# Cross-attention and routed experts on one core: exponentials per head on ScalarE, and both halves of the expert weights split with one pass fewer, the low half on VectorE

## The reference

```
x = x + softmax(mask(Wq·LN(x) · (Wk·ctx)^T / 8)) · (Wv·ctx) · Wo + bo        16 heads of 64
h = LN(x);  s = sigmoid(h·gate^T + bias);  the two largest of 9 experts per token, weights normalised
x = x + sum over the two experts e:  cw[e] · (silu(h·w1[e]^T) * (h·w3[e]^T)) · w2[e]^T     hidden width 704
```

## Time and profile before

| | us |
|---|---|
| median of 3 runs | 498.68 |
| lowest, highest | 497.95, 504.11 |
| the profiled execution | 499.68 |
| its span, first to last instruction | 497.8 |

### The profile page before, as it was taken

How to read it: one execution, slowest core, us unless ns; L and a number is a source line. 1 busy time by engine, 2 the same in 40 slices (tenths; PEclk the granted TensorE clock), 3 DMA queues, 4 the chain that set the end, 5 groups by cost and what they waited for, 6 DMA issues and landing times.

```text
span 497.8 us, 11324 instructions
## 1 busy us (share of the span) xinstructions
PE 409.8 (82%) x3049; PEld 310.2 (62%) x3049; DVE 315.9 (63%) x714; ACT 242.2 (49%) x402; POOL 294.5 (59%) x269
## 2 busy tenths in 40 slices
PE   2868769999999998721139999999999999999970
PEld 3758347786686686611015777777777777777750
DVE  5883689998898888459954745455545545544430
ACT  2877257877777783187214343334334333343310
POOL 0232166988988987374733655676666666666232
PEclk9979889999999999965557999999999999999986
DMA  8902773465466465245223878999999999999751
GB/s 264 339 4 85 232 244 111 136 193 201 134 191 200 135 182 181 69 130 154 69 69 81 158 137 135 142 141 139 133 150 132 142 144 139 137 137 155 113 82 22
DMA packets 112610, 71.45 MB, mean 144 GB/s; under 512 B 82940, under 2 KB 106172, under 8 KB 112572
## 3 DMA queue, kind: packets, MB, share of 16 engines
q1 hardware_dynamic: 104892, 60.43, 53.2%
q0 software_dynamic: 7680, 10.49, 13.9%
HBM read 39.02 MB, written 12.22 MB: 103 GB/s over the span
## 4 chain that ended last, share of the span: by engine, by line
PE 52%; DVE 15%; DMA 12%; POOL 8%; issue 6%; ACT 4%; SPq 1%; POOLq 1%; DVEq 0%; ACTq 0%
PE ps L611 29%; PE ps L624 14%; DMA out_rows<-work 8%; POOL w_all L1134 4%; POOL work L1146 2%; PE ps L479 2%; PE ps L448 2%; DVE work L878 2%; DVE work L1051 1%; DMA w_all<-in_wk 1%; PE ps L528 1%; DVE work L885 1%; DMA w_all<-b_rows 1%; DVE work L900 1%; PE ps L592 1%
## 5 line engine op out<-in xcount | busy, mean ns | idle before, releaser
L611 PE MATMUL ps<-w_all,work 128*128 x960 | 152.2, 316 | 8.9 <-DMA work<-work 8.9
L611 PEld LDWEIGHTS ps<-w_all,work 128*128 128x128 f16 x960 | 94.9, 99 | 57.1 <-issue 9.1
L1206 POOL DMA_INDIRECT out_rows<-work x40 | 64.1, 1602 | 57.7 <-DMA out_rows<-work 21.4
L1087 DVE SCALAR_TENSOR_TENSOR work<-ps,work 128x352 f32<-128x352 f32 x80 | 42.0, 524 | 70.7 <-PE ps L611 70.7
L624 PE MATMUL ps<-w_all,work 128*128 x680 | 82.1, 276 | 2.7 <-DMA work<-work 2.7
L1134 POOL TENSOR_TENSOR w_all<-stage,w_all 128x1088 f16<-128x1088 f32 (+1 forms) x32 | 74.5, 2333 | 6.8 <-ACT w_all L702 6.8
L1194 POOL DMA_INDIRECT work<-xn_rows,work x40 | 58.5, 1462 | 33.2 <-POOL work L1191 32.2
L624 PEld LDWEIGHTS ps<-w_all,work 128*128 128x128 f16 x680 | 67.2, 99 | 14.4 <-issue 2.9
L779 ACT ACTIVATE work<-work 128x704 f16<-128x704 f32 x40 | 31.6, 790 | 77.3 <-DVE work L1087 77.3
L528 PE MATMUL ps<-w_all,work 128*128 128x256 f16 (+1 forms) x480 | 55.1, 273 | 9.2 <-DVE work L910 9.2
L773 ACT ACTIVATE work<-ps 128x352 f32<-128x352 f32 x80 | 36.9, 464 | 46.9 <-PE ps L611 46.5
(11 more groups left out here) (135 smaller groups left out, 575.5 us busy)
## 6 DMA issues: line engine op xcount, KB each, us to landing
stage<-in_wt SPq DMA_DIRECT2D x36, 544.0 KB, 4.2
work<-in_x SPq DMA_DIRECT2D x32, 128.0 KB, 4.3
b_rows<-w_all SPq DMA_DIRECT2D x4, 616.0 KB
w_all<-b_rows SPq DMA_DIRECT2D x2, 1152.0 KB, 5.8
out_rows<-work SPq DMA_DIRECT2D x17, 128.0 KB, 5.0
xn_rows<-work SPq DMA_DIRECT2D x17, 128.0 KB, 4.3
w_all<-in_x SPq DMA_DIRECT2D x1, 2048.0 KB, 15.6
work<-work SPq DMA_TRANSPOSE x80, 3.4
```

What stands on the lines that cost most here:

```text
L611: mm = pe.matmul(ps[:, c, 0:half], xt[:, par, block, :], weights(wbase + off, half), start=(k == 0 and n == 0), stop=(k == KD - 1 and n == 2))
L1087: dve.scalar_tensor_tensor(out=sg[:, par, c * HID // 2:(c + 1) * HID // 2], in0=ps[:, 2 + c, 0:HID // 2], scalar=1.0 / SP_W, in1=sg[:, par ...
L1206: pool.indirect_dma_start(out=acc, out_offset=bass.IndirectOffsetOnAxis(ap=ids[:, par], axis=0), in_=yb[:, par], in_offset=None, compute_o ...
```

## The change

For the experts 0 to 5 ScalarE now writes the high half straight from the loaded chunk, in one pass with scale 64 (`w_direct`), and does not scale `stage` in place. The low half, 64 times `stage` minus high half, is made by VectorE in one instruction (`w_rest`), two per step in steps 4 to 15, behind `normalise2` and ahead of `logits`. GpSimd's two `w_low` per step are gone from the token loop; for the experts 6 and 7 the old way stays.

VectorE no longer subtracts the maxima from the scores. It multiplies them by -1/8 (`nmx`, three instructions of 128 x 6 or 128 x 4). ScalarE makes the exponentials from PSUM, head by head: 16 instructions of 128 x 77 with the head's column of `nmx` as bias and an accumulator output that gives the head's sum. VectorE's sum over `ebuf` is gone; its reciprocal stays. The score banks are released by the exponentials.

```diff
--- before.py
+++ after.py
@@ -153,6 +153,7 @@
         xn2b, o = view(work, o, [2, D], F32)
         xn2t, o = view(work, o, [2, KD, P], F32)
         mx, o = view(work, o, [2, HEADS], F32)
+        nmx, o = view(work, o, [2, HEADS], F32)
         rs, o = view(work, o, [2, HEADS], F32)
         rr, o = view(work, o, [2, HEADS], F32)
         st6, o = view(work, o, [2, 6], F32)
@@ -247,8 +248,8 @@
         x_in, xr_in = sems("x_in", 2), sems("xr_in", 2)
         x1_out, xn2_out = sems("x1_out", 2), sems("xn2_out", 2)
         xn_ok, xt_mm, xh_ok, xl_ok, sc_mm = (sem(n) for n in ("xn_ok", "xt_mm", "xh_ok", "xl_ok", "sc_mm"))
-        max_ok, sub_ok, exp_ok, sum_ok, rec_ok, norm_ok = (sem(n) for n in (
-            "max_ok", "sub_ok", "exp_ok", "sum_ok", "rec_ok", "norm_ok"))
+        max_ok, neg_ok, exp_ok, rec_ok, norm_ok = (sem(n) for n in (
+            "max_ok", "neg_ok", "exp_ok", "rec_ok", "norm_ok"))
         pt_mm, ph_ok, pl_ok, out_mm, xb_ok, x1_ok = (sem(n) for n in ("pt_mm", "ph_ok", "pl_ok", "out_mm", "xb_ok", "x1_ok"))
         st_ok, mv_ok, ve_ok, rstd_ok, xn2_ok = (sem(n) for n in ("st_ok", "mv_ok", "ve_ok", "rstd_ok", "xn2_ok"))
         xn2t_mm, xn2t_ok, gate_mm, lg_ok = (sem(n) for n in ("xn2t_mm", "xn2t_ok", "gate_mm", "lg_ok"))
@@ -497,7 +498,7 @@
                 pe.wait_ge(xl_ok, i + 1)
                 h0 = 0
                 for c, nh in enumerate(SC_H):
-                    at_least(pe, sub_ok, 3 * i + (c - 2))
+                    at_least(pe, exp_ok, 3 * i + (c - 2))
                     w = nh * J
                     dst = ps[:, c, 0:w]
                     pe.matmul(dst.rearrange("p (h j) -> p h j", j=J), idb[:],
@@ -698,8 +699,13 @@
                     act.wait_ge(w_in[part], e * 16 + 16)
                     act.activation(stage[:, part, :], stage[:, part, :], ACT.Copy, scale=SP_W).then_inc(w_sc_ok, 1)
                 for part in parts:
-                    act.wait_ge(w_sc_ok, e * 4 + (part + 1))
+                    act.wait_ge(w_sc_ok, (e - EARLY) * 4 + (part + 1))
                     act.activation(w_chunk(e, part, 0), stage[:, part, :], ACT.Copy).then_inc(w_hi_ok, 1)
+
+            def w_direct(e, parts):
+                for part in parts:
+                    act.wait_ge(w_in[part], e * 16 + 16)
+                    act.activation(w_chunk(e, part, 0), stage[:, part, :], ACT.Copy, scale=SP_W).then_inc(w_hi_ok, 1)
 
             def x_high(i, par):
                 act.wait_ge(xt_mm, i + 1)
@@ -707,8 +713,17 @@
                 act.activation(x_h[:, par], ps[:, 7, 0:D].rearrange("p (k t) -> p k t", k=KD), ACT.Copy).then_inc(xh_ok, 1)
 
             def exp(i, par):
-                act.wait_ge(sub_ok, 3 * i + 3)
-                act.activation(ebuf[par][:, 0:HJ], ebuf[par][:, 0:HJ], ACT.Exp, scale=DH ** -0.5).then_inc(exp_ok, 1)
+
+                at_least(act, pt_mm, 3 * (i - 1))
+                at_least(act, rec_ok, i - 1)
+                h = 0
+                for c, nh in enumerate(SC_H):
+                    act.wait_ge(neg_ok, 3 * i + (c + 1))
+                    for k in range(nh):
+                        ins = act.activation(ebuf[par][:, h * J:(h + 1) * J], ps[:, c, k * J:(k + 1) * J], ACT.Exp,
+                                             bias=nmx[:, par, h:h + 1], scale=DH ** -0.5, accum_out=rs[:, par, h:h + 1])
+                        h += 1
+                    ins.then_inc(exp_ok, 1)
 
             def p_high(i):
                 at_least(act, out_mm, i)
@@ -737,7 +752,7 @@
                     for b in range(B):
                         act.wait_ge(b_out[b], 16 * 2)
                 if on_w(n):
-                    w_high((s - W_STEP) // 2, chunk_parts(n))
+                    w_direct((s - W_STEP) // 2, chunk_parts(n))
                 if on(n, LAG_G):
                     gate_copy(s - LAG_G, (n - LAG_G) % 2)
                 if on(n, 0):
@@ -879,18 +894,20 @@
 
             def shift(i, par):
 
-                at_least(dve, pt_mm, 3 * (i - 1))
+                at_least(dve, exp_ok, 3 * (i - 1))
                 for c, (h0, nh, src) in enumerate(score_banks()):
                     dve.wait_ge(max_ok, 3 * i + (c + 1))
-                    dve.tensor_tensor(ebuf[par][:, h0 * J:(h0 + nh) * J].rearrange("p (h j) -> p h j", j=J), src,
-                                      mx[:, par, h0:h0 + nh].unsqueeze(2).to_broadcast([P, nh, J]),
-                                      ALU.subtract).then_inc(sub_ok, 1)
+                    dve.tensor_scalar(nmx[:, par, h0:h0 + nh], mx[:, par, h0:h0 + nh], -DH ** -0.5, None,
+                                      ALU.mult).then_inc(neg_ok, 1)
+
+            def w_rest(e, parts):
+                for part in parts:
+                    dve.wait_ge(w_hi_ok, e * 4 + (part + 1))
+                    dve.scalar_tensor_tensor(out=w_chunk(e, part, 1), in0=stage[:, part, :], scalar=SP_W,
+                                             in1=w_chunk(e, part, 0), op0=ALU.mult, op1=ALU.subtract).then_inc(w_lo_ok, 1)
 
             def sums(i, par):
-                dve.wait_ge(exp_ok, i + 1)
-                dve.tensor_reduce(rs[:, par], ebuf[par][:, 0:HJ].rearrange("p (h j) -> p h j", j=J), AX.X,
-                                  ALU.add).then_inc(sum_ok, 1)
-                dve.wait_ge(sum_ok, i + 1)
+                dve.wait_ge(exp_ok, 3 * i + 3)
                 at_least(dve, norm_ok, i - 1)
                 dve.reciprocal(rr[:, par], rs[:, par]).then_inc(rec_ok, 1)
 
@@ -959,6 +976,8 @@
                     normalise(s + 2, n % 2)
                 if on(n, LAG_XN2):
                     normalise2(s - LAG_XN2, (n - LAG_XN2) % 2)
+                if on_w(n - 1):
+                    w_rest((s - 1 - W_STEP) // 2, chunk_parts(n - 1))
                 if on(n, LAG_G):
                     logits(s - LAG_G)
                 if n in B_STEPS:
@@ -1158,12 +1177,8 @@
             def step(s, n):
                 if on(n, 2):
                     bias(s - 2, n % 2)
-                if on_w(n - 1):
-                    w_low((s - 1 - W_STEP) // 2, chunk_parts(n - 1)[0])
                 if on(n, 1):
                     norm(s - 1, (n - 1) % 2)
-                if on_w(n - 1):
-                    w_low((s - 1 - W_STEP) // 2, chunk_parts(n - 1)[1])
                 if n in B_STEPS:
                     b_low(n - B_STEPS[0])
                 if n == LATE_SPLIT + 2:
```

## The result

| | before | changed |
|---|---|---|
| median, us | 498.86 (4 runs) | 544.07 (4 runs, 543.49 to 545.99) |
| profiled execution's span, us | 497.8 | 542.3 |
| mean granted TensorE clock | 0.923 | 0.907 |

The ratio is 1.0889, 95% interval 1.0809 to 1.0969: the change makes the kernel slower by 45 us.

A forecast was written before the change was run, and what follows sets the result against it. TensorE was taken as nearly the bound, 8.87 of 9.24 us a step, waiting for residual behind a store. After the change: 499.68 + 34.6 (ring) + 1.2 (steps 1 to 3) = 535.5, forecast 535 us, range 519 to 556.

The forecast's parts named there:

- the ring: Token loop: residual, VectorE's low halves, weight loads, store, next residual; bounds each of 12 steps, +34.6 us in all.
- the first steps: Steps 1 to 3, set by ScalarE: 3 x 0.4 = 1.2 us slower, at most 11.
- First part of the ring: VectorE from residual to the end of both low halves: 2.15 + 0.40 + 0.79 + 2.47 = 5.81 us.
- the third rival: GpSimd holds up VectorE's w_rest by 0.4 to 1.2 us per step, 10 us in all: 545 us; chance 0.10.
- Second part: SyncE's queue and store, low halves' end to next residual: 6.56 us in hardware loop, 5.8 in written-out steps, 6.31 mean.
- my lower end: ScalarE's exponentials overlap and start every 0.12 us, 1.9 us per tile.
- my upper end: ScalarE reads each exponential's accumulator with an extra instruction: 0.49 us each, 7.8 us per tile.
- ScalarE's ring: Residual, maxima and first product, exponentials, probabilities' split, halves of x, next residual: 8.8 us, costing nothing in steps 4 to 15.
- The first one: SyncE's weight loads don't hold up the store; TensorE's 8.87 us a step bounds, 495 us; chance 0.05.
- The second: ScalarE becomes the bound at 0.6 us an exponential, 13.9 us a step: 572 us; chance 0.03.
- The fourth: TensorE's clock falls in its new waits, about 14.9 us a step: 568 us; chance 0.04.
- the row with 3.09 us: Earlier trace row: a TensorE wait of 3.09 us left the granted clock at 1.00, so it should hold.

The follow-up runs named there:

- cut in two different ways: Changed kernel with VectorE's low halves first in its step: 511.64 us; changed kernel with SyncE's store ahead of the weight loads: 514.16 us.
- one reordering: Changed kernel with only SyncE's queue reordered, the weight loads issued one step later, behind that step's store: 514.16 us, ratio 1.0247.
- the full reordering: Kernel before with SyncE's weight loads behind the store of x1 and ahead of the store of the normalised rows: 494.16 us, ratio 0.9866.
- the first reordering tried there: Kernel before with SyncE's two weight loads behind both stores of the step, ahead of the residual tile's load: 503.61 us, ratio 1.0051.

## Why the prediction was right, and where its sizes were off

I said 535 us, range 519 to 556, slower with 0.93; it is 544.07. The mechanism, the ring, holds: it is in the chain, it is cut in two different ways with the same result, and it is there without the exponentials. The sum is 9 us short of the profiled execution (544.35): 4.0 us in the ring, 3.5 in the first steps and 1.2 behind step 16, where I had nothing (from `residual` of step 16 to that of step 17 it takes 8.55 us in place of 7.03; I did not look for the cause).

**First part of the ring, 5.81 us forecast.** It comes to 149.45 less the twelve second parts (77.3 us), over 12: 6.01 us. VectorE in step 7 and step 8:

```profile
134.19 0.30 DVE L900 TENSOR_SCALAR work<-work 128x6 f32<-128x6 f32 x3
134.45 0.18 DVE L939 BATCH_NORM_AGGREGATE work<-work 128x2 f32<-128x6 f32 x1
135.56 3.02 DVE L906 SCALAR_TENSOR_TENSOR w_all<-stage,w_all 128x1088 f32 x2
...
147.37 0.29 DVE L900 TENSOR_SCALAR work<-work 128x6 f32<-128x6 f32 x3
...
148.70 2.49 DVE L906 SCALAR_TENSOR_TENSOR w_all<-stage,w_all 128x1088 f32 x2
```

The three products took 0.30, not 0.40, but in the hardware loop VectorE also idles 0.24 us ahead of L874, which I had not counted; up to the low halves it is 3.35 us on average, as forecast (3.34). The two low halves took 2.49 in eight steps, as forecast (2.47), and 3.02 in steps 4 to 7. That is the third rival, in part: GpSimd's bias sum had just started in step 7, and in step 8 it started just after VectorE.

```profile
135.50 0.73 POOL L1169 TENSOR_TENSOR work<-work,bo_b 128x256 f32<-128x256 f32 x1
...
148.84 2.93 POOL L1169 TENSOR_TENSOR work<-work,bo_b 128x256 f32<-128x256 f32 x1
```

Step 6 is like step 7. In steps 4 and 5 the sum started 0.46 us into the first low half, got its turn between the two and held up the second:

```profile
97.31 1.41 POOL L1169 TENSOR_TENSOR work<-work,bo_b 128x256 f32<-128x256 f32 x1
98.05 1.82 DVE L906 SCALAR_TENSOR_TENSOR w_all<-stage,w_all 128x1088 f16<-128x1088 f32 x1
```

Together it cost 4 x 0.53 = 2.1 us. The Trainium skill, page "SBUF — State Buffer", section "SBUF: two separate sides", says that the first of the two keeps the other out for its whole instruction. Steps 7 and 4 agree: VectorE loses 0.53 us to a sum that takes 0.73. In step 8 the sum lasts 2.93 us and ends 0.58 after VectorE's second low half, so it was kept out for two instructions, where the rule speaks of one. What decides between the two cases no run shows.

**Second part, 6.31 forecast.** 77.3 / 12 = 6.44 us: 6.6 in the hardware loop as said, 6.17, 6.26, 5.86 and 6.06 at the written-out steps where I took 5.8. Together with the first part 12 x 0.33 = 4.0 us, +38.6 in place of +34.6.

**The first steps, +1.2 forecast: the mis-sized term.** They cost 4.7 us. An exponential costs 0.30 us, near the 0.28 taken (the 0.12 of my lower end stood on no row), but it is two instructions, as my upper end had it (ScalarE, order of time):

```profile
147.88 0.32 ACT L723 ACTIVATE w_all<-ps,work 128x77 f32<-128x77 f32 x1
148.08 0.20 ACT L723 ACTIVATION_READ_ACCUMULATOR w_all<-ps,work 128x1 f32 x1
148.18 0.32 ACT L723 ACTIVATE w_all<-ps,work 128x77 f32<-128x77 f32 x1
```

What I had too short was ScalarE's ring: step 3 to step 4 takes 93.72 - 83.90 = 9.82 us, not 8.8. From `residual` to the first exponential it is 2.4 us (2.3 taken), the exponentials take 4.8 (4.5), and from ScalarE's split at 91.12 to the next `residual` it is 2.6, where I had 2.0. The slower exponentials count from tile 1 on, so that `residual` of step 3 is already 83.90 - 80.62 = 3.3 us late. This last number is rough: `residual` of step 3 starts at 82.17 to 84.30 in the six traces with the accumulators, and at 80.62 to 82.37 in the five with the exponentials as before, 1.8 us apart on average. So of the 4.7 us some 3.2 are the exponentials' and the rest may be the difference of one trace from another. Without the accumulators step 3 to step 4 takes 8.36 us.

**The rivals.** The first one (not slower) had the store free of the low halves; it is not. The second needed 0.49 us an exponential; it is 0.30. The third cost 2.1 us where I had 10. The fourth: I said the clock would stay at 1.00. It did not. These are a wait and the `project` behind it, twice (columns as in the earlier trace rows):

```profile
155.72:158.55 2.83, 0.00 (x1) 0.01 (x1) 0.72 (x2) 1.27 (x2) 0.00 (x0) 0.91 0.28 101
158.55:163.00 4.45, 4.45 (x28) 3.44 (x29) 4.21 (x12) 2.94 (x20) 2.41 (x3) 0.67 0.10 29
143.07:145.94 2.87, 0.00 (x1) 0.01 (x1) 0.72 (x2) 1.38 (x2) 0.00 (x0) 1.00 0.17 62
145.94:149.00 3.06, 3.06 (x28) 2.75 (x29) 2.82 (x11) 1.44 (x11) 1.03 (x3) 1.00 0.14 43
```

After one wait of 2.8 us the granted clock was 0.67, part of the stretch at the lower of the two levels (1.2 and 2.4 GHz), after another of the same length 1.00. Of the twelve waits for `residual` in steps 5 to 16, eight were followed by such a fall (the waits 2.1 to 4.6 us), four were not (1.3 to 2.9 us), so the length of the wait alone does not decide it. The Trainium skill, page "TensorE: Matmul & The Clock Gate", section "HAM oscillation — how this bites in real kernels", which I had set aside for the row with 3.09 us, describes such falls after waits for DMAs that come back in every turn; the waits in its example are longer than most here. The fall cost nothing here: the step from 157.83 with the slow `project` took 12.55 us, the one from 145.22 with the fast one 12.61. That TensorE's spare 3.3 us took it up fits this.

## What to carry to other kernels

Before moving work from one engine to another, ask not only whether the new engine has the time, but what stands ahead of the work in its order and what waits for its result: here 2.5 us of work moved behind the one instruction that waits for a store, while the queue of that store waits for the work. That made a ring of two lines of code that never name each other. A queue that serves several engines in order carries every wait to all that is behind it, and its order is the cheapest thing to change: one reordering took back 30 of the 45 us, and in the kernel before, the full reordering gave 1.3%. But the first reordering tried there only put another wait in front; read what each entry of the queue waits for.

## What the runs showed of the hardware that was not expected

- A VectorE instruction with two SBUF inputs and a GpSimd one kept each other out: 0.73 us of GpSimd's work took 2.93 us beside two low halves when VectorE was just ahead, and 1.41 us when it started later in the first of them and got in between; the low halves took 3.02 in place of 2.49 us when GpSimd was first or got in between.
- An exponential of 128 x 77 with accumulator output is an ACTIVATE and a read of the accumulator, 0.30 us for both, 4.8 us for 16, against 1.23 us for one ACTIVATE of 128 x 1232. Without the accumulator output 16 of them took 3.55 us.
- The granted clock fell after some waits of TensorE of 2.1 to 2.9 us that came back every 12.5 us or so, and not after others of 1.3 to 2.9 us.
- The time from the low halves' end to `residual` fell from 6.6 to between 4.5 and 6.2 us when the two loads ahead of the store were issued further apart.
